# The front's normalized tokens: halves split in rows and turned by transposing transfers, in place of TensorE transposes

## Time and profile before

| | us |
|---|---|
| median of three runs | 1765.65 |
| fastest, slowest run | 1765.45, 1768.32 |
| the profiled execution | 1766.67 |
| span of its instructions | 1764.7 |
| TensorE busy | 1631.4 (92%) |
| VectorE busy | 1212.8 (69%) |
| ScalarE busy | 937.1 (53%) |
| GpSimd busy | 234.3 (13%) |

### The profile page before, as it was taken

The page is one execution under the profiler, slowest core; times in us unless marked ns, Lnnn a source line. Parts: engine busy times, 40 slices in busy tenths (PEclk is TensorE's granted clock), DMA queues, the critical chain, the costliest instruction groups (busy, mean ns, idle before and its releaser), DMA issues.

```text
span 1764.7 us, 31065 instructions
## 1 busy us (share of the span) xinstructions
PE 1631.4 (92%) x12304; PEld 987.9 (56%) x12304; DVE 1212.8 (69%) x2544; ACT 937.1 (53%) x1378; POOL 234.3 (13%) x296
## 2 busy tenths in 40 slices
PE   1579999899999999999999999999999999999998
PEld 0333567536665467644765457653666446754566
DVE  6775775857767676757758577676776767685743
ACT  2315655366544665456553565546654566535655
POOL 3021112011020113001030110201111011301100
PEclk9668999999999999999999999999999999999999
DMA  4221002010021002010020100201011100200000
GB/s 129 91 54 37 1 1 64 2 46 1 4 61 46 1 1 54 11 46 1 1 64 2 46 1 1 64 10 37 1 30 36 46 1 2 64 2 10 1 10 10
DMA packets 25095, 48.08 MB, mean 27 GB/s; under 512 B 7411, under 2 KB 16819, under 8 KB 23573
## 3 DMA queue, kind: packets, MB, share of 16 engines
q1 hardware_dynamic: 15840, 28.63, 5.9%
q0 software_dynamic: 6144, 9.45, 2.3%
q10 hardware_dynamic: 2966, 8.01, 1.3%
HBM read 20.70 MB, written 6.29 MB: 15 GB/s over the span
## 4 chain that ended last, share of the span: by engine, by line
PE 69%; DVE 22%; ACT 4%; issue 3%; DMA 1%; POOL 1%; SPq 0%; DVEq 0%; ACTq 0%
PE ps L428 19%; PE ps L704 16%; PE ps L651 13%; PE ps L462 7%; DVE mx L1154 7%; PE ps L585 3%; DVE acc L1310 3%; DVE room L1326 3%; PE ps L505 2%; DVE norm_stats L995 1%; PE ps L435 1%; PE ps L492 1%; PE ps L465 1%; ACT room L867 1%; DVE gn_st L1037 1%
## 5 line engine op out<-in xcount | busy, mean ns | idle before, releaser
L867 ACT ACTIVATE room<-ps,b_sb 128x512 f32<-128x512 f32 x384 | 263.2, 685 | 464.4 <-PE ps L428 463.2
L704 PE MATMUL ps<-wout_h,room 128*128 128x192 f16 x3072 | 462.9, 247 | 5.4 <-DVE acc L1310 5.4
L1326 DVE SCALAR_TENSOR_TENSOR room<-room 128x512 f16<-128x512 f32 x384 | 263.4, 689 | 177.9 <-ACT room L873 172.9
L704 PE MATMUL ps<-wout_l,room 128*128 128x192 f16 x1536 | 379.7, 247 | 0.0
L845 ACT ACTIVATE room<-ps 128x1024 f32<-128x1024 f32 (+3 forms) x288 | 229.7, 811 | 174.8 <-PE ps L465 119.9
L704 PEld LDWEIGHTS ps<-wout_h,room 128*128 128x128 f16 x3072 | 288.2, 98 | 44.5 <-DVE acc L1310 11.8
L1154 DVE TENSOR_REDUCE mx<-ps 128x2 f32<-128x1024 f32 (+3 forms) x288 | 265.6, 951 | 42.7 <-PE ps L585 20.3
L873 ACT ACTIVATE room<-room 128x512 f16<-128x512 f32 x384 | 241.9, 630 | 34.3 <-PE ps L704 0.7
L651 PE MATMUL ps<-room,v 128*64 128x512 f32 (+3 forms) x1152 | 246.7, 511 | 0.0
L585 PE MATMUL ps<-qk 96*128 96x512 f16 (+3 forms) x576 | 160.8, 351 | 38.4 <-DVE mx L1154 29.8
L704 PEld LDWEIGHTS ps<-wout_l,room 128*128 128x128 f16 x1536 | 151.1, 98 | 27.9 <-issue 0.8
(11 more groups left out here) (210 smaller groups left out, 2375.5 us busy)
## 6 DMA issues: line engine op xcount, KB each, us to landing
xc<-x_ch SPq DMA_DIRECT2D x8, 768.0 KB, 5.7
qk<-qk_all SPq DMA_DIRECT2D x96, 64.0 KB, 2.4
qk<-qk_all POOLq DMA_DIRECT2D x96, 64.0 KB, 2.5
out<-acc ACTq DMA_DIRECT2D x16, 384.0 KB, 2.7
xt<-x_tok SPq DMA_DIRECT2D x7, 768.0 KB, 7.1
qk<-qk_all POOLq DMA_DIRECT2D x96, 32.0 KB, 2.0
qk<-qk_all SPq DMA_DIRECT2D x96, 32.0 KB, 2.3
room<-w_in SPq DMA_DIRECT2D x2, 1024.0 KB, 10.9
```

The source lines that it names most:

```text
L704: mm = pe.matmul(dst, hid[:, s, tok], w[:, n, :], start=(k == 0 and m == 0 and t % 2 == 0), stop=False, skip_group_check=True)
L867: act.activation(h32[:, i % N_H, :], ps[:, H_BANK[i], :], ACT.Gelu, scale=1 / (U_SCALE * W_SCALE), bias=b1_sb[:, n:n + 1])\
L1326: V.scalar_tensor_tensor(out=h_l[:, s, :], in0=h32[:, s, :], scalar=A_SCALE, in1=h_h[:, s, :], op0=ALU.mult, op1=ALU.subtract)\
```

## The change

The halves are made from the tokens as they lie, before any transposition, and turned as fp16 by transposing transfers that SyncE issues:

- The 16 TensorE transposes per image of the front go, with their semaphore `a_tr`. Those of the tail (layer 3's tokens) stay.
- ScalarE writes the high half from u in SBUF into `rows16`, VectorE the low half from u and that. `rows16` is [128 tokens, 8 tiles, 2 halves, 256] fp16 and lies in the first 4096 columns of `qk_all`, the place of q and k, so ScalarE first waits for the spreads of the image before.
- SyncE's new `turn`, ahead of `spread`: per block it waits for the low half and issues four transposing transfers, one for each tile of 128 tokens, 512 columns (128 KB) each, which write the four 128x128 squares of `a16` (`ah` and `al` are its halves).
- TensorE waits ahead of its first q/k projection for the transfers of both blocks; the waits for the low halves go.

```diff
--- before.py
+++ after.py
@@ -182,13 +182,14 @@
         t1 = sb("t1", [P, NT, C], F32)
         acc = sb("acc", [P, NT, C], F32)
         u = sb("u", [P, NT, 2 * P], F32)
-        ah = sb("ah", [P, 2, N], F16)
-        al = sb("al", [P, 2, N], F16)
+        a16 = sb("a16", [P, 4, N], F16)
+        ah, al = a16[:, 0:2, :], a16[:, 2:4, :]
         uh = sb("uh", [P, 2, N], F16)
         ul = sb("ul", [P, 2, N], F16)
 
 
         qk_all = sb("qk_all", [P, 2 * QK_PARTS * N], F16)
+        rows16 = qk_all[:, 0:NT * 4 * P].rearrange("p (t half c) -> p t half c", t=NT, half=2)
         qk = qk_all[:, :].rearrange("p (half j n) -> p half j n", half=2, j=QK_PARTS)
 
 
@@ -308,7 +309,7 @@
         p_ps = sem("p_ps", NT // 2)
         t1_ready = sem("t1_ready", 1)
         a_ready = sem("a_ready", NB)
-        a_tr = sem("a_tr", NB)
+        turned = [sem("turned0", 16 * TB), sem("turned1", 16 * TB)]
         ah_done = sem("ah_done", NB)
         al_done = sem("al_done", NB)
         qk_ps = sem("qk_ps", QK_PARTS * NB)
@@ -375,6 +376,15 @@
                 sp.wait_ge(t1_ready, at(t1_ready, img, 0))
                 sp.dma_start(xt[:, :, :], x_tok[img]).then_inc(x_tok_in, 16)
 
+            def turn(img):
+
+                for b in range(NB):
+                    sp.wait_ge(al_done, at(al_done, img, b + 1))
+                    for t in range(b * TB, (b + 1) * TB):
+                        sp.dma_start_transpose(a16[:, :, t * P:(t + 1) * P],
+                                               rows16[:, t, :, :].rearrange("p half c -> p (half c)"))\
+                          .then_inc(turned[b], 16)
+
             def spread(img):
 
 
@@ -410,8 +420,10 @@
                 sp.dma_start(stage[:, n % 2, 0:w], src).then_inc(stage_in[n % 2], 16)
 
             for img in range(B - 1):
+                turn(img)
                 spread(img)
                 load(img + 1)
+            turn(B - 1)
             spread(B - 1)
 
 
@@ -538,15 +550,14 @@
                         mm.then_inc(p_ps, 1)
 
 
-                for b in range(NB):
-                    yield FRONT_AT["turn"] + b + 0.5
-                    pe.wait_ge(a_ready, at(a_ready, img, b + 1))
-                    transpose_block(b, 4 + 2 * b).then_inc(a_tr, 1)
+                yield FRONT_AT["turn"] + 1.5
                 for i in range(QK_PARTS * NB):
                     b, j = divmod(i, QK_PARTS)
                     yield FRONT_AT["qk"] + i // 2 + (0.5 if i % 2 else 0)
 
-                    pe.wait_ge(al_done, at(al_done, img, 1 if i < 2 else 2))
+                    if i == 0:
+                        for b2 in range(NB):
+                            pe.wait_ge(turned[b2], at(turned[b2], img, whole(turned[b2])))
                     if i >= 4:
                         pe.wait_ge(qk_lo, at(qk_lo, img, i - 3))
                     project(ps[:, 4 + i % 4, :], ah, al, slice(COL_QK + j * P, COL_QK + (j + 1) * P),
@@ -775,8 +786,12 @@
 
                 for b in range(NB):
                     yield FRONT_AT["high"] + b
-                    act.wait_ge(a_tr, at(a_tr, img, b + 1))
-                    act.activation(ah[:, :, b * QB:(b + 1) * QB], ps[:, 4 + 2 * b:6 + 2 * b, :],
+                    if b == 0 and later:
+                        for b2 in range(NB):
+                            act.wait_ge(heads_in[b2], at(heads_in[b2], img, 0))
+                            act.wait_ge(keys_in[b2], at(keys_in[b2], img, 0))
+                    act.wait_ge(a_ready, at(a_ready, img, b + 1))
+                    act.activation(rows16[:, b * TB:(b + 1) * TB, 0, :], u[:, b * TB:(b + 1) * TB, :],
                                    ACT.Copy, scale=U_SCALE).then_inc(ah_done, 1)
                 for i in range(QK_PARTS * NB):
                     b, j = divmod(i, QK_PARTS)
@@ -1134,9 +1149,9 @@
                 for b in range(NB):
                     yield FRONT_AT["low"] + b
                     dve.wait_ge(ah_done, at(ah_done, img, b + 1))
-                    V.scalar_tensor_tensor(out=al[:, :, b * QB:(b + 1) * QB],
-                                           in0=ps[:, 4 + 2 * b:6 + 2 * b, :], scalar=U_SCALE,
-                                           in1=ah[:, :, b * QB:(b + 1) * QB], op0=ALU.mult,
+                    V.scalar_tensor_tensor(out=rows16[:, b * TB:(b + 1) * TB, 1, :],
+                                           in0=u[:, b * TB:(b + 1) * TB, :], scalar=U_SCALE,
+                                           in1=rows16[:, b * TB:(b + 1) * TB, 0, :], op0=ALU.mult,
                                            op1=ALU.subtract).then_inc(al_done, 1)
                 for i in range(QK_PARTS * NB):
                     b, j = divmod(i, QK_PARTS)
```

## The result

The changed kernel takes 1872.97 us (median of 4 runs, 1869.84 to 1875.55), the kernel before beside it 1766.84 us: a ratio of 1.06, 95% interval 1.058 to 1.062. It is 106 us slower. Forecast were 1879 us and a range of 1810 to 2060.

A forecast was written before the change was run, and what follows sets the result against it. TensorE was taken as the bound. A 14.2 us loss in each of seven later images (99 us) plus 13.4 us in image 0 gave 113 us on 1766.67, so 1880, or 1879 as timed median; range 1810 to 2060.

The forecast's parts named there:

- What bounds the kernel: Whole kernel: TensorE is the bound, busy in 92% of the 1764.7 us span and still for 133 us.
- The halves' times: Front inside the expert loop: VectorE's order ends block 0's low half at 269.1 and block 1's at 272.2.
- ScalarE's part: High halves made from SBUF instead of PSUM: same 1.02 us per block, ahead of VectorE's need, no cost.
- The join: Ahead of the first projection TensorE waits for both blocks' transfers, not only block 0's, so the whole expert loop stands still.
- The price of a transfer: Each of SyncE's eight transposing transfers per image: 1.5 us in the queue and 3.25 us to landing.
- the middle value: SyncE's queue time per transposing transfer: 1.5 us, the geometric middle between 0.65 and 3.4 us.
- the upper one: High queue price per transfer: 3.4 us, from 512 pieces, 32 per DMA engine at 0.105 us each.
- The clock: After the stall TensorE runs 2.9 us at half speed, costing 1.45 us on the projections.
- image 0: No expert loop to stop, but the wait is on the path: first projection 12.0 us later, 13.4 us with the clock.
- Nothing given back: Behind the front VectorE and ScalarE have no backlog to work off during the stall, so no time is recovered.
- Rival 2: Transposing transfers don't pipeline, 5.7 us each: 46 us per later image, 2133 us in all; chance 0.17.
- rival 3: Delay made good behind the front, freed 2.6 us per image stay: 1747 us; chance 0.05.

The follow-up runs named there:

- E3: Changed kernel with TensorE's first two projections waiting for block 0's transfers alone, the other four for block 1's: 1826.1 us (ratio 1.0331).
- E7: Kernel before with one wait moved: the first two projections wait for the low halves of both blocks: 1803.26 us (ratio 1.0213).
- E1: Changed kernel with each transposing transfer split into two of half the columns (64 KB), same bytes in all: 1951.95 us (ratio 1.105).
- E5: Changed kernel with one transposing transfer per two tiles (256 KB), four per image in place of eight: 1838.12 us (ratio 1.0399).
- E2: Changed kernel with plain copies of the same bytes in place of the transposing transfers, tokens left unturned: 1831.57 us (ratio 1.0368).
- E6: Changed kernel with one transposing transfer per block (512 KB), two per image: 1827.54 us (ratio 1.0338).
- E4: Changed kernel with 55 unread filler matmuls on TensorE ahead of the transfer wait in the seven expert loops: 1850.34 us (ratio 1.0479).
- E12: E10's kernel with image 0's tokens turned by TensorE as in the kernel before: 1760.01 us (ratio 0.9957).
- E9: Changed kernel with one transfer per block, waits by block, q/k projections from step 29, v 33, maxima 36 at 3.0 per chunk: 1796.78 us (ratio 1.0164).
- E10: Changed kernel with one transfer per block, waits by block, q/k projections from step 28, v 32, maxima 35.5 at 2.9 per chunk: 1766.48 us (ratio 0.9993).

## Why the prediction was right

**What bounds the kernel: right.** TensorE's work stayed what it was and its order decided. It stands still for 102 us more (235 against 133 us), nearly all of it in the wait for the transfers, and the loss is 106.

**The halves' times: right.** VectorE's order gave 269.1 and 272.2; the changed trace has 269.07 and 272.11. The claim that ScalarE's part costs nothing held too: from SBUF a high half takes 1.04 to 1.06 us against 1.02 from PSUM, and VectorE never waits for it.

**The join: right, and it is nearly half of the loss.** E3 takes 47 us off by parting it. In the kernel before it costs 35 us alone (E7), 32 us in the traced run.

**The price of a transfer: mechanism right, size off.** I took 1.5 us in the queue and 3.25 to landing; it is 1.27 and 2.5, which puts the first projection 10.94 us late (292.09 - 11.25 = 280.84 against 269.90) in place of 12.95. My reason for the middle value was wrong: pieces per DMA engine don't set it (E1 halves them at 1.25 us each), the issue of each transfer does, from 64 to 256 KB (E1, E5). That 1.5 us came close to 1.27 is luck: it is the middle of two bounds, and the upper one measures something else. It is twice the issue of a plain copy (E2).

**The two rules on transposing transfers.** The Trainium skill ("VectorE: DVE Perf Modes", The three transpose paths) gives 1309 ns for one 128x128 by the crossbar. It does not say whether that is time in the queue or to landing. Here a transfer of two squares takes 1.25 us of the queue and one of eight 1.32 us: the figure agrees with the queue time as a price per transfer, and not as one per square, for which E5 and E6 would have been no faster than the changed kernel. The Trainium skill ("Advanced Engine Details and Errata", X-Bar Transpose (TRN2)) has transposing transfers as fast as regular ones: of the landing that holds (2.5 against 2.4 us), of the queue it does not (1.27 against 0.65).

**The clock: too small.** I took 2.9 us at half speed from the earlier trace rows; it was 4.5 us in the mean of the seven loops, 2.25 us of loss in place of 1.45. E4 bears it out, with the later falls of the clock counted apart. The set-up's rows showed where the clock rises after one resumption, not how long it may stay low. The two errors run against each other: 10.94 - 0.2 + 2.25 = 13.0 us per image against 14.2 forecast, and 13.1 measured. For image 0 I had 13.4, it was 12.5. Part of the closeness of 1879 to 1873 is that luck.

**Nothing given back: right.** The waits for the maxima are 30.3 us against 29.8. Rival 2 (5.7 us each, one after another) fell with the 1.27 us, rival 3 with these waits. Of rival 3's 18 us E12 reaches 7, with the order changed as well, and most of them by the clock.

## What to carry to other kernels

Moving work from a busy engine to a transfer pays only where other work of that engine stands between the transfer's issue and its use; here 2.6 us per image of transposes were traded for 13 us of stillness. Count such a wait with the clock: 3.2 us of stillness in the middle of the loop cost 4.2 us per image in E7's trace (212.4 against 208.2). If cover is made by moving steps, look at what is crowded at the other end, and give a transposing transfer as much as one pattern can describe, since from 64 to 256 KB its issue costs nearly the same here (1.25 to 1.32 us). And before a gain of a few us is put down to the work removed, compare images at the same clock: of E12's gain most was the clock's.

## What the runs showed of the hardware that I had not expected

- A transposing transfer inside SBUF holds SyncE's queue 1.25, 1.27, 1.32 and 1.86 us (medians) at 64, 128, 256 and 512 KB; a plain copy of 128 KB 0.65 us.
- A stillness of 3.22 us, in a loop that is else almost fully busy, was enough for the granted clock to fall, and it falls after the work has resumed (E7: the first matmul at 276.75 still at full speed, those from 277.26 on at 0.63 us).
- The clock also fell with no such stillness before it: in E9 at 342.5 us, behind waits of 1.28 and 0.53 us. In E10, behind waits of 1.27 and 0.51 us at the same place in the program, it did not. So the length of the waits alone does not tell whether it falls.
- Matmuls whose result nobody reads made the kernel 22.6 us faster (E4; 18.8 us between the profiled executions).
